# The small constant of two norms added by two-column sums on VectorE, in a fused eight-layer block on one core

## The reference, cut to what matters

```python
def _layernorm(x, axis=-1, eps=1e-05):
    m = jnp.mean(x, axis=axis, keepdims=True)
    v = jnp.var(x, axis=axis, keepdims=True)
    return (x - m) / jnp.sqrt(v + eps)
...
x = x + 0.5 * _L0_ffn_ref(_layernorm(x, axis=-1), ...)
x = x + _L0_attn_ref(_layernorm(x, axis=-1), ...)
x = x + 0.5 * _L0_ffn_ref(_layernorm(x, axis=-1), ...)
```

## Time and profile before

| what | value |
|---|---|
| median of 3 runs | 2673.2 us |
| time of the profiled execution | 2674.05 us |
| its span in the trace | 2672.3 us |
| mean granted TensorE clock | 0.99 of full |
| PE, DVE, ACT, POOL busy | 2574.2, 2413.6, 2334.2, 2054.6 us |
| PE and DVE share of the chain that ended last | 63% and 21% |

### The profile page before, as it was taken

How to read it: one execution, slowest core, us unless ns; L and a number is a source line. 1 busy time by engine, 2 the same in 40 slices (tenths; PEclk the granted TensorE clock), 3 DMA queues, 4 the chain that set the end, 5 groups by cost and what they waited for, 6 DMA issues and landing times.

```text
span 2672.3 us, 80386 instructions
## 1 busy us (share of the span) xinstructions
PE 2574.2 (96%) x29048; PEld 2073.9 (78%) x29048; DVE 2413.6 (90%) x6523; ACT 2334.2 (87%) x7345; POOL 2054.6 (77%) x2185
## 2 busy tenths in 40 slices
PE   5999999999999999998999999999999999999998
PEld 4778778877888888885777688777887788888876
DVE  7999999999999999985777999999999999999995
ACT  4899999999999999994444899999999999999996
POOL 7998889988888888771102999998998877888873
PEclk9999999999999999998999999999999999999999
DMA  3111111111111111110000111111111111111111
GB/s 99 47 49 28 31 36 30 29 28 39 27 29 28 32 37 31 28 33 1 3 7 2 32 29 28 30 38 28 28 27 37 29 28 38 39 35 40 35 32 33
DMA packets 63812, 83.95 MB, mean 31 GB/s; under 512 B 11538, under 2 KB 30652, under 8 KB 63420
## 3 DMA queue, kind: packets, MB, share of 16 engines
q1 hardware_dynamic: 63420, 78.82, 12.8%
HBM read 11.67 MB, written 4.19 MB: 6 GB/s over the span
## 4 chain that ended last, share of the span: by engine, by line
PE 63%; DVE 21%; ACT 10%; issue 4%; POOL 1%; DMA 0%; SPq 0%; DVEq 0%; ACTq 0%; POOLq 0%
PE PS L654 6%; PE PS L670 6%; PE PS L644 5%; PE PS L620 5%; PE PS L611 5%; PE PS L613 4%; PE PS L612 4%; ACT P L4495 4%; PE PS L734 3%; DVE SS L2151 3%; DVE T L2162 3%; PE PS L715 2%; DVE SQ L2170 2%; PE PS L803 2%; DVE MX L2205 2%
## 5 line engine op out<-in xcount | busy, mean ns | idle before, releaser
L4495 ACT ACTIVATE P<-PS,MX 128x128 f32<-128x128 f32 x2048 | 768.0, 463 | 7.0 <-DVE MX L2205 6.2
L5791 POOL TENSOR_TENSOR T<-T,SQ 128x512 f32<-128x512 f32 x512 | 653.8, 1283 | 60.5 <-DVE SQ L2170 53.2
L5827 POOL TENSOR_TENSOR P<-P,RI 128x512 f32<-128x512 f32 x512 | 527.3, 1042 | 117.3 <-DVE RI L2211 117.3
L4495 ACT ACTIVATION_READ_ACCUMULATOR P<-PS,MX 128x1 f32 x2048 | 568.9, 302 | 0.0
L5804 POOL TENSOR_TENSOR T<-T,RN 128x512 f32<-128x512 f32 x512 | 520.8, 1046 | 11.9 <-DVE RN L2199 11.4
L4502 ACT COPY PT<-PS 128x512 f32<-128x512 f32 x512 | 315.1, 697 | 77.7 <-PE PS L654 77.4
L4450 ACT ACTIVATE SQ<-PS 128x512 f32<-128x512 f32 x512 | 346.1, 678 | 34.6 <-PE PS L613 23.2
L2162 DVE TENSOR_TENSOR T<-PS,TAB 128x512 f32<-128x512 f32 x512 | 349.5, 684 | 17.4 <-ACT SQ L4450 12.4
L2151 DVE TENSOR_REDUCE SS<-SQ 128x8 f32<-128x512 f32 x512 | 341.4, 675 | 26.2 <-ACT SQ L4450 22.6
L611 PE MATMUL PS<-WH,YH 128*128 128x512 f32 x768 | 343.4, 447 | 10.4 <-DVE SQ L2170 4.5
L2170 DVE TENSOR_TENSOR SQ<-PS,TAB 128x512 f32<-128x512 f32 x512 | 347.7, 680 | 3.4
(11 more groups left out here) (129 smaller groups left out, 5996.3 us busy)
## 6 DMA issues: line engine op xcount, KB each, us to landing
VP<-VP SPq DMA_DIRECT2D x480, 128.0 KB, 2.3
out_dram<-X SPq DMA_DIRECT2D x16, 256.0 KB, 3.0
X<-in_L_attn_x_dram SPq DMA_DIRECT2D x7, 512.0 KB, 4.6
SG<-in_L_ffn_w_dram SPq DMA_DIRECT2D x5, 341.0 KB, 3.2
SG<-in_L_ffn_wqkv_dram SPq DMA_DIRECT2D x4, 384.0 KB, 3.4
SGQ<-in_L_ffn_wqkv_dram SPq DMA_DIRECT2D x4, 256.0 KB, 3.4
X<-in_table_dram SPq DMA_DIRECT2D x2, 512.0 KB, 5.9
P<-in_L_ffn_wo_dram SPq DMA_DIRECT2D x2, 256.0 KB, 3.0
```

Source lines behind the costliest of these rows:

```text
L4495: ins = act.activation(P[:, g, p, :], PS[:, b, 128 * p:128 * p + 128], ACT.Exp, bias=MX[:, g, p:p + 1], accum_out=SM[:, g, p:p + 1])
L5791: pool.tensor_tensor(T1[:, k, :], T1[:, k, :], SQ[:, (2 * n + 1 - x) % 3, :], ALU.add).then_inc(added[x], 1)
L5827: pool.tensor_tensor(P[:, g], P[:, g], RI[:, g, :].unsqueeze(2).broadcast_to([128, NPAIR, 128]), ALU.mult).then_inc(p_scaled, 1)
```

## The change

MV and RMV get a third column, which two new memsets fill with EPS once at the start. The scalar addition of EPS (L2119 and L2257) becomes a `tensor_reduce` with an addition over columns 1 and 2 (variance and EPS), written to new tiles VE and RVE instead of in place. The negated mean (L2258) becomes a `tensor_reduce` with `negate=True` over one column. POOL's readers take VE and RVE. The two new memsets come ahead of the others, so every threshold of `dve_set` that stood for the old ones rises by two, and the two reductions wait for `dve_set` at 2. The order of all queues stays the same otherwise.

```diff
-    RMV = sb("RMV", [2 * TPC, 2])
+    RMV = sb("RMV", [2 * TPC, 3])
+    RVE = sb("RVE", [2 * TPC])
+    VE = sb("VE", [8])
...
-    MV = sb("MV", [8, 2])
+    MV = sb("MV", [8, 3])
...
-                    on.wait_ge(dve_set, 3)
+                    on.wait_ge(dve_set, 5)
...
-            on.wait_ge(dve_set, 2)
+            on.wait_ge(dve_set, 4)
...
-                dve.bn_aggr(MV[:, m + i, :], ST[:, m + i, :]).then_inc(ln_mean, 1)
+                dve.bn_aggr(MV[:, m + i, 0:2], ST[:, m + i, :]).then_inc(ln_mean, 1)
...
+            on.wait_ge(dve_set, 2)
             on.wait_ge(ln_mean, TPC * outer(t))
-            dve.tensor_scalar(MV[:, m:m + 2, 1:2], MV[:, m:m + 2, 1:2], EPS, None, ALU.add).then_inc(ln_var, 1)
+            dve.tensor_reduce(VE[:, m:m + 2], MV[:, m:m + 2, 1:3], AX.X, ALU.add).then_inc(ln_var, 1)
...
         def rows_eps(u):
+            on.wait_ge(dve_set, 2)
             on.wait_ge(row_mean, 2 * TPC * (u + 1))
-            dve.tensor_scalar(RMV[:, :, 1], RMV[:, :, 1], EPS, None, ALU.add).then_inc(row_var, 1)
-            dve.tensor_scalar(RNM[:], RMV[:, :, 0], -1.0, None, ALU.mult).then_inc(row_var, 1)
+            dve.tensor_reduce(RVE[:], RMV[:, :, 1:3], AX.X, ALU.add).then_inc(row_var, 1)
+            dve.tensor_reduce(RNM[:], RMV[:, :, 0:1], AX.X, ALU.add, negate=True).then_inc(row_var, 1)
...
+        dve.memset(MV[:, :, 2:3], EPS).then_inc(dve_set, 1)
+        dve.memset(RMV[:, :, 2:3], EPS).then_inc(dve_set, 1)
         dve.memset(NHALF[:], -0.5).then_inc(dve_set, 1)
...
-            pool.tensor_tensor(RSB[:, 0, :], RMV[:, :, 1], NHALF[:], ALU.pow).then_inc(rstd, 1)
+            pool.tensor_tensor(RSB[:, 0, :], RVE[:], NHALF[:], ALU.pow).then_inc(rstd, 1)
...
-                ins = pool.tensor_scalar(XN[:, i, :], X[:, n + i, :], MV[:, m + i, 0:1], MV[:, m + i, 1:2], ALU.subtract,
+                ins = pool.tensor_scalar(XN[:, i, :], X[:, n + i, :], MV[:, m + i, 0:1], VE[:, m + i:m + i + 1], ALU.subtract,
                                          ALU.mult)
...
-            v = MV[:, m:m + 2, 1]
+            v = VE[:, m:m + 2]
             pool.tensor_tensor(v, v, NHALF[:, 0:2], ALU.pow).then_inc(ln_rstd, 1)
```

More of the change, by code:

```diff
@@ L2252, in rows_aggregate @@
                 on.wait_ge(row_stat, n * u + i + 1)
-                dve.bn_aggr(RMV[:, i, :], RST[:, i, :]).then_inc(row_mean, 1)
+                dve.bn_aggr(RMV[:, i, 0:2], RST[:, i, :]).then_inc(row_mean, 1)
         def rows_eps(u):
+            on.wait_ge(dve_set, 2)
             on.wait_ge(row_mean, 2 * TPC * (u + 1))
-            dve.tensor_scalar(RMV[:, :, 1], RMV[:, :, 1], EPS, None, ALU.add).then_inc(row_var, 1)
-            dve.tensor_scalar(RNM[:], RMV[:, :, 0], -1.0, None, ALU.mult).then_inc(row_var, 1)
+            dve.tensor_reduce(RVE[:], RMV[:, :, 1:3], AX.X, ALU.add).then_inc(row_var, 1)
+            dve.tensor_reduce(RNM[:], RMV[:, :, 0:1], AX.X, ALU.add, negate=True).then_inc(row_var, 1)
         def rest_of_hn(u):
@@ L5830, in row_rstd @@
         def row_rstd(u):
-            on.wait_ge(dve_set, 1)
+            on.wait_ge(dve_set, 3)
             on.wait_ge(row_var, 2 * (u + 1))
             on.wait_ge(rows_normed, u)
-            pool.tensor_tensor(RSB[:, 0, :], RMV[:, :, 1], NHALF[:], ALU.pow).then_inc(rstd, 1)
+            pool.tensor_tensor(RSB[:, 0, :], RVE[:], NHALF[:], ALU.pow).then_inc(rstd, 1)
             on.wait_ge(rstd, u + 1)
```

## The result

The changed kernel takes 2665.59 us (median of 11 runs, 2664.68 to 2668.64) against 2672.8 us of the kernel before in the same session (11 runs, 2671.27 to 2675.55): 7.2 us less, ratio 0.9972, 95% interval 0.9964 to 0.998. The forecast was 2666.7 us, a gain of 6.5. The profiled execution has a span of 2663.8 us, 8.5 us less than that of before.

The account below looks back on a forecast made before the run. PE binds for about 17 us of each steady first-layer pair, DVE for about 20 us. Gains of 3.4 + 2.6 + 0.5 = 6.5 us from 2673.2 us gave 2666.7 us, range 2662.0 to 2673.5 us.

Parts of the forecast that it names:

- L2119's price: Outer norm's EPS addition on DVE: mean 419 ns because it waits for POOL, 0.16 us with POOL idle; a reduction never waits.
- the ceiling: Pipeline fillings: six L2119 on the chain, together 4.8 us against some 0.5 us unblocked, so 4.3 us gain at most.
- The price of small reductions: New DVE reductions in both norms: 157 ns at 4 elements and 161 ns at 8, bounds about 0.15 us and 286 ns.
- rival of dear reductions: DVE's part of steady pairs: small reductions take 286 ns each, giving 2678 us, or 2680 without the fillings; chance 0.08.
- rival that the change does nothing: Outer norm: the small reduction waits for POOL too, L2119 stays at 0.42 us, time at 2673 us; chance 0.07.
- Term 1: Steady pairs, L2119 in DVE's part: 13 of 23 blocked, 0.26 us saved in each, 3.4 us in all.
- Term 2: Steady pairs, L2119 in PE's part: blocked 0.2 to 0.4 us each, gain nothing, hidden by PE.
- Term 3: Pipeline fillings after the start and the attention: 60% of at most 4.3 us, 2.6 us gain.
- Term 4: Inner norm's L2257 and L2258: 0.02 us shorter in each of some 27 pairs where DVE binds, 0.5 us gain.
- more than the chain shows: Steady pairs give 4.7 us, fillings all 4.3, inner norm another microsecond: some 10 us, 2663 us; chance 0.10.
- only the steady pairs pay: Filling stalls are covered by ACT and POOL, leaving 3.4 + 0.5 us gain, 2669.3 us; chance 0.22.

Follow-up runs that it names:

- experiment 4: Changed kernel plus a 128-column reduction on DVE behind the outer norm's addition: in every second steady pair 2665.33 us, in every steady pair 2665.84 us.

## Why the prediction was right, and where its steps were not

- **L2119's price is a wait for POOL, and a reduction doesn't pay it: right.** Means of 419, 424 and 381 ns for the three forms that wait, 148 ns for the one that does not. One thing in the reading of all 64 is not so: the L2119 at 147.80 us comes up 0.04 us before L5827 ends and then sits through a whole L5791 as well, 1.31 us in all. It was in the ceiling all the same, as 0.51 us of the chain.
- **The price of small reductions: right.** 161 and 148 ns measured, 161 and 157 ns forecast. The rival of dear reductions and the rival that the change does nothing are both dead by these rows. (The dear rival's own terms add up to 5.2 us and not 4.6, and "no small operation of this trace is near" 65 ns leaves out the memsets of 59 to 62 ns; neither bears on the forecast.)
- **Term 1, the steady pairs, 3.4 us: too large.** The traces show 0.6 us per half, 1.2 us in all (1.0 and 2.0 us with the outer norm alone). The failed step is the sentence that nothing absorbs the gain there. DVE's part did become 0.25 us shorter in each blocked pair, and PE's wait did go to 0.79 us in both kinds, as forecast. But the forecast took the pair behind, at 36.87 us, as the undisturbed length, and it was not: it was short because the delay before it had let ACT get ahead. Both kinds came out at 37.02 us, near the old mean of 37.05. The 0.36 us between the two kinds of pair was the stall and its repayment together, and the part that I had put down to the memset of VP was mostly the repayment: the addition in every second pair brings 37.12 and 36.87 us back, while all pairs without stall or addition last 37.0 us with the memset still there in every second one.
- **Term 2, L2119 in PE's part, nothing: right** as far as can be seen. DVE's wait for PE's transposes is 0.60 us as before.
- **Term 3, the fillings, 2.6 us: too small.** The traces give 3.8 and 2.3 us at the two places in the profiled pair. The start of pair 2 comes at 171.9 to 174.0 us in five traces with scalar additions and at 170.2 to 171.8 us in five with reductions, leaving out four (two of each kind, 1.3 us apart) in which the granted clock was at its lower level for 20 us from about 22 us on: 1.8 us by their means, with single profiles of the two kinds up to 2.1 us apart among themselves. With 1.7 us from the second filling that is 3.5 us of the ceiling of 4.3 us. I had discounted the ceiling to 60% since ACT, POOL and PE take turns there; it was 80%. The 60% rested on no row; where the chain is shown above, POOL, DVE and PE wait for one another in turn, so that there was little slack to cover a stall.
- **Term 4, the inner norm, 0.5 us: not there.** By its own prices the two operations save 0.034 us together and not 0.02, 0.9 us over 27 pairs, and even so the runs show nothing. The kernel without it takes 2664.08 us and the changed one 2665.59 and 2665.82. The second layer's pairs are 36.30 us with the shorter operations and 36.26 us on average before (but 36.29 us too in the kernel with both fillings, whose inner norm is scalar). By the mechanism of experiment 4 a slightly shorter DVE isn't worth anything there; that it costs a microsecond is not shown, as the runs overlap.
- **Not in the forecast: the clock.** Pair 30's 1.4 us and some part of the second filling. The stalls by the traces give 3.5 + 1.2 = 4.7 us; with pair 30 it is 6.1 us, and the medians say 7.2. The remaining microsecond lies within the measurement (the interval of the ratio, 0.9964 to 0.998, is 2.1 us to either side).
- **The rival "more than the chain shows"** had the fillings right and the steady pairs wrong; "only the steady pairs pay" was the opposite of what happened.

So the total was right to 1.1 us with a term too large by 2.2 us, one too small by 0.9 us, one of 0.5 us that was not there, and a share of the clock that was not thought of. The operation that stalls and the one that doesn't were read rightly; that the sum came out so near is luck. The stalls alone come to 4.7 us, below the 5.3 us that a measurement can tell; the chance of 0.55 for a gain over 0.2% would have had to be lower with the right terms.

## What to carry to other kernels

A tiny operation with a mean of several hundred nanoseconds is waiting inside itself: compare it with neighbours of its kind and size, and put another engine's timeline beside its end; then look for an operation with the same result that does not wait. Price its removal first where the pipeline fills, where no engine has slack. In a steady loop, a pair that is short right behind a long one is not the undisturbed length, and the mean of the two is what the loop takes; adding the suspected cost back as plain work is the quickest test of whether it ever counted, provided that you read from the next dependent step how much of the added work really delays the engine.

## What the runs showed of the hardware that was not expected

**A wait for POOL can outlast several of its instructions.** In the kernel with the inner norm alone, DVE and POOL over 1488 to 1495 us:

```profile
1488.68 3.03 POOL L5833 TENSOR_TENSOR P<-P,RI 128x512 f32<-128x512 f32 x3
...
1490.31 2.65 DVE L2122 TENSOR_SCALAR VE<-MV 128x2 f32<-128x2 f32 x1
1491.68 1.26 POOL L5797 TENSOR_TENSOR T<-T,SQ 128x512 f32<-128x512 f32 x1
...
1494.37 1.28 POOL L5797 TENSOR_TENSOR T<-T,SQ 128x512 f32<-128x512 f32 x1 [1.43 <-DVE SQ L2173]
```

L2122 starts at 1490.31 beside the second of three L5833 (about 1.0 us each) and ends at 1492.96, 0.02 us after L5797's 1492.94, with two ends of POOL instructions in between. POOL then stood 1.43 us, waiting for DVE. The forecast had read that such an operation ends with the POOL instruction that is running when it comes up, and 44 of the 45 L2119 over 0.2 us do so in the kernel before, 28 of them although POOL's next instruction follows at once. So DVE does not have to wait for a gap in POOL's work as a rule, and what decides who comes next is not shown. The one that doesn't, 1.31 us at 147.80 us, outlasts one end, and has its like (1.27 to 1.31 us) in every trace without reductions there. The 2.65 us stand in the third profile of before too, and in the kernel with the steady pairs alone. These are the three traces with scalar additions in the second filling and no lower clock from 1482 us on; in the four that have the lower clock there, the longest scalar or two-operand addition of the second filling takes 0.72 to 1.25 us. A single two-float operation can cost 2.65 us, and what it costs went along with the clock of another engine here.

**The granted clock differs between executions of the same kernel.** The stretches from about 22, 45 to 55, 1205 and 1482 us on at which it is at its lower level come and go. In the four traces with 20 us of it from 22 us on, pair 2 starts some 3 us later than in the others of their kind. A mean granted clock of 0.987 went with 2675.0 us in 9 runs of the kernel before, one of 0.992 with 2672.6 us in 15 runs, about half a microsecond per thousandth. At 0.992 the changed kernel has 2665.4 us in 4 runs: the gain at equal mean clock is 7.3 us there, and 5.6 to 7.4 us at 0.989 to 0.991, so a difference of mean clocks doesn't explain it. A mean doesn't say where the lower clock lies, though, and pair 30 shows that the place counts.
